# Expert logits as three products: x's part before attention, the projection's part in 8 extra columns, new routing groups

## The chip, the cores and the metric

The kernel runs on 1 core of one Trainium2 chip. The metric is the device time of one launch in microseconds (us). Before the change it is 968.08 us, the median of 3 runs (967.9 to 970.68). The engines are TensorE (PE in the profile, its weight loads PEld), VectorE (DVE), ScalarE (ACT), GpSimd (POOL) and SyncE (SP), which here issues most of the transfers.

## The reference

One layer of attention and a feed-forward part with 8 experts, over 4 x 1024 tokens of width 256, in float32:

```
x2  = x + proj(attention(rope(qkv(layernorm(x)))))       # 16 heads of 16, causal
xn  = layernorm(x2)
aff = xn @ centroids.T                                    # 8 logits for each token
e   = argmax(aff);  alpha = sigmoid(aff[e])
h   = relu((layernorm(xn) * ln_g[e] + ln_b[e]) @ w1[e].T + b1[e])
out = x2 + alpha * (xn + h @ w2[e].T + b2[e]) + (1 - alpha) * xn
```

What matters here is `aff`. The mean of a token is a shift that centred centroids cancel and its standard deviation is a positive factor, so the largest logit can be found from x2 times the centred centroids. As x2 = x + o @ w_proj + b, those logits are the sum of x @ c, o @ (w_proj @ c) and b @ c.

## The kernel before, in words

There are four stages, each a block in which every engine has its own instruction list in program order, tied to the others by semaphores.

**Projection** (`phase_project_attend`, h = 0 to 15): 8 blocks of 512 tokens, two steps h each. x and its transpose x_feat are loaded in rings of three (`xt`, `xf`; `load_x`, `load_features`, XR = 3). PE projects q and k (line 970) and v (line 892), DVE applies the rotation and splits into three bf16 parts together with ACT and POOL; POOL's `part3` is the last part of step h, after which SP's `store(h)` writes the parts to DRAM (line 511). From h = 11 on PE already computes score blocks for the first attention step ("items", `put_item`, line 944), and DVE reduces each to block maxima (line 800). Items 9 to 17 follow after the last step (the drain). There are 18 items for a step; items 11 to 14 are the diagonal ones. SP's loads of the q and k stacks for the attention steps 0 and 1 are spread over h = 5 to 7 and h = 12 to 15.

**Attention** (16 steps of one batch and four heads): the maxima are transposed (line 913), split on DVE (779, 781) and POOL, and stored as extra rows of the stack by SP (line 556); then the scores (line 1004), exponentials on ACT (line 712), masks on POOL (line 636) and the product with v (line 1020). The items of the next step stand between the scores, by a plan written in `ITEM_AT` and `FIRST_AT`. POOL loads the experts' second weights in steps 1, 2, 14 and 15.

**Routing** (`phase_route`): 32 tiles of 128 tokens. For tile n, PE transposes o (line 1404), ACT copies it (`oT`, line 1212), PE adds the bias row (line 1395) and the projection (line 1397) in `ps_p`, and DVE adds x (line 1317). Then PE transposes x2 (line 1418), ACT copies it (`xT`, line 1218) and PE multiplies it by the centred centroids (`ps_a`, line 1427), which were made at the start of the stage (line 1409, DVE 1241). PE's order in iteration n is: bias and projection of tile n+1, transposes of o of tile n+2, transposes of x2 of tile n-1, logits of tile n-2. The tiles are in groups, GROUPS = (8, 8, 8, 4, 4). Per group DVE finds the expert (`one_hot`), PE counts ranks (1434, 1436), DVE makes row numbers (`positions`) and scales; ACT writes the first half of the payload (`scaled`, 1203), DVE the second (`tail`, 1310), and POOL scatters one tile per instruction to its expert's region in DRAM (line 1194). At the end DVE makes the table of slots (lines 1344 to 1381); SP then loads the first expert's weights and, after all scatters, the first rows (line 216). SP also stores pad rows at the regions' ends.

**Experts** (`phase_ffn`): 39 slots of 128 rows, not touched by the change.

## Time and profile before

| what | value |
|---|---|
| median of the runs | 968.08 us (967.9 to 970.68) |
| the profiled execution | 968.24 us, its span 966.3 us |
| mean granted PE clock | 0.962 of 2.4 GHz |
| busy in the span | PE 896.1, DVE 610.3, ACT 532.7, POOL 313.8 us |
| DMA | 130.41 MB, mean 135 GB/s |
| projection, attention, routing, experts | to about 124, to 569, to 670, to 966 us |

The busy time of PE is over 90% of the span, yet this is an average over stages: at the two passages, from projection to attention and from routing to the experts, PE waits for others.
### The profile page before, as it was taken

Reading aid. Unit: us, or ns where it says so; the run is one execution under the profiler, and the core shown is the slowest. Engines: PE = TensorE matmul, PEld = TensorE weight load, DVE = VectorE, ACT = ScalarE, POOL = GpSimd, SP = SyncE. Lnnn points to the kernel's source line nnn. Section 1 sums busy time; section 2 is a strip of 40 time slices with the busy share of each in tenths; the row PEclk is TensorE's granted clock in tenths of the full one; section 3 lists DMA queues with packets and bytes.
Section 4 is the critical chain, followed back from the end, with each engine's and each line's share of the span. In section 5 each row is a group of like instructions: output and inputs, shape, how many; then the busy total and the mean of one; then the engine's idle time right before and its main releaser. Section 6 shows DMA issues by size and latency. Waiting matters only on the chain. (4 is left out here: it accounts for less than half of the span.)

```text
span 966.3 us, 20566 instructions
## 1 busy us (share of the span) xinstructions
PE 896.1 (93%) x6695; PEld 540.2 (56%) x6696; DVE 610.3 (63%) x1107; ACT 532.7 (55%) x1339; POOL 313.8 (32%) x470
## 2 busy tenths in 40 slices
PE   7998769999999999999999879962999999999996
PEld 4554313333333333333333238851999999999996
DVE  5989989888888888888887015772232332332332
ACT  4666428778777778777878834560323223223221
POOL 9987734322233323232233310452011111111111
PEclk9999869999999999999999989985999999999998
DMA  7694543322222211112242036336565665665660
GB/s 258 218 246 162 155 137 120 123 68 68 68 67 67 68 55 52 48 50 68 68 154 88 3 121 197 122 148 202 182 212 188 199 212 185 199 213 186 198 216 7
DMA packets 54891, 130.41 MB, mean 135 GB/s; under 512 B 9761, under 2 KB 30626, under 8 KB 48546
## 3 DMA queue, kind: packets, MB, share of 16 engines
q1 hardware_dynamic: 49234, 107.93, 36.1%
q0 software_dynamic: 5584, 21.54, 5.9%
q8 instruction: 43, 0.70, 0.3%
q14 instruction: 30, 0.25, 0.1%
HBM read 100.95 MB, written 28.48 MB: 134 GB/s over the span
## 5 line engine op out<-in xcount | busy, mean ns | idle before, releaser
L712 ACT ACTIVATE arena<-ps_pair 128x512 f32<-128x512 f32 (+3 forms) x768 | 328.9, 494 | 103.3 <-PE ps_pair L1004 98.7
L800 DVE TENSOR_REDUCE B_block_max<-ps_item 128x8 f32<-128x1024 f32 x288 | 340.6, 1221 | 41.5 <-PE ps_item L944 38.3
L1004 PE MATMUL ps_pair<-q_stack,k_stack 99*128 99x512 bf16 (+7 forms) x768 | 191.0, 333 | 5.2 <-ACT arena L712 2.9
L636 POOL TENSOR_SCALAR_AFFINE_SELECT arena<-arena 128x256 f32<-128x256 f32 x256 | 103.9, 406 | 202.8 <-ACT arena L712 200.5
L1020 PE MATMUL ps_pair<-arena,B_v_quad 128*32 128x512 f32 (+3 forms) x1536 | 163.6, 498 | 1.0 <-ACT B_oacc L726 0.7
L1004 PEld LDWEIGHTS ps_pair<-q_stack,k_stack 99*128 99x128 bf16 (+1 forms) x768 | 54.0, 97 | 187.7 <-ACT arena L712 170.5
L1602 PEld LDWEIGHTS D_ps_h<-D_xT,arena 128*128 128x128 f32 x1248 | 147.9, 195 | 4.7 <-ACT D_xT L1540 2.8
L1602 PE MATMUL D_ps_h<-D_xT,arena 128*128 128x128 f32 x1248 | 148.5, 278 | 2.1 <-ACT D_xT L1540 2.1
L1621 PE MATMUL D_ps_y<-arena,D_hr 128*128 x624 | 141.0, 379 | 0.0
L1531 ACT ACTIVATE D_hr<-D_ps_h,ffn_columns 128x128 f32<-128x128 f32 x156 | 44.5, 368 | 165.1 <-PE D_ps_h L1602 165.1
L1621 PEld LDWEIGHTS D_ps_y<-arena,D_hr 128*128 128x128 f32 x624 | 115.7, 190 | 14.1
L1514 POOL DMA_INDIRECT out<-D_res,D_ids x39 | 38.4, 984 | 262.2 <-issue 200.9
L944 PE MATMUL ps_item<-k_stack,q_stack 64*128 64x128 bf16 (+2 forms) x1280 | 107.0, 269 | 14.6 <-DVE B_block_max L800 9.7
L1561 DVE TENSOR_SCALAR D_hr<-D_ps_h,ffn_columns 128x128 f32<-128x128 f32 x156 | 43.9, 345 | 115.3 <-PE D_ps_h L1602 115.3
L944 PEld LDWEIGHTS ps_item<-k_stack,q_stack 64*128 64x128 bf16 x1280 | 46.6, 96 | 68.7 <-DVE B_block_max L800 31.5
L1576 DVE TENSOR_TENSOR D_y<-D_ps_y,ffn_bias 128x256 f32<-128x256 f32 x39 | 16.6, 425 | 84.1 <-PE D_ps_y L1621 84.1
L1540 ACT ACTIVATE D_xT<-D_ps_x,ffn_columns 128x128 f32<-128x128 f32 x78 | 31.4, 453 | 53.6 <-PE D_ps_x L1611 53.6
L970 PE MATMUL ps_pair<-arena 128*128 128x512 f32 x128 | 57.9, 595 | 0.2 <-DVE arena L768 0.2
L1020 PEld LDWEIGHTS ps_pair<-arena,B_v_quad 128*32 128x32 f32 x1536 | 30.3, 108 | 36.2 <-ACT arena L712 15.8
L1194 POOL DMA_INDIRECT payload<-C_pay,C_posi x32 | 31.3, 978 | 57.9 <-DVE C_pay L1310 37.9
L583 POOL TENSOR_TENSOR arena<-arena 128x512 f32<-128x512 f32 x32 | 48.8, 1542 | 2.2 <-DVE arena L841 2.1
L841 DVE SCALAR_TENSOR_TENSOR arena<-ps_pair,A_bq,arena 128x512 f32<-128x512 f32 x64 | 43.6, 739 | 1.8 <-PE ps_pair L970 1.8
(149 smaller groups left out, 786.8 us busy)
## 6 DMA issues: line engine op xcount, KB each, us to landing
arena<-in_w_exp SPq DMA_DIRECT2D x39, 1024.0 KB, 5.1
qk_parts<-arena SPq DMA_DIRECT2D x32, 384.0 KB, 3.4
q_stack<-qk_parts SPq DMA_DIRECT2D x96, 128.0 KB, 2.9
rows<-payload SPq DMA_DIRECT2D x39, 257.0 KB, 2.7
arena<-in_x SPq DMA_DIRECT2D x16, 512.0 KB, 6.4
k_stack<-qk_parts SPq DMA_DIRECT2D x64, 128.0 KB, 2.9
arena<-in_w_exp POOLq DMA_DIRECT2D x8, 1024.0 KB, 6.6
arena<-in_x_feat SPq DMA_DIRECT2D x8, 512.0 KB, 5.8
```

The costliest lines, as they stand in the source:

```text
L583: pool.tensor_tensor(rot[:, h % 2, c, :], rot[:, h % 2, c, :], ds[:, h % 2, 1 - c, :], op).then_inc(s_rot, 1)
L636: pool.affine_select(out=block_p, in_=block_p, compare_op=ALU.is_ge, fill=0.0, base=0, pattern=[[0, 2], [1, P]], channel_multiplier=-1).th ...
L712: act.activation(pr[s % PR][:, h, 0:QW - off], ps_s[(QH * s + j) % R][:, 0:QW - off], ACT.Exp, scale=scale).then_inc(s_e, 1)
L800: dve.tensor_reduce(bmx[:, g:QH:GH, first:first + 3 * gap + 1:gap], src[:, :, :].rearrange("p c (b n) -> p c b n", n=P), AX.X, ALU.max).th ...
L944: mm = pe.matmul(dst[:, half, at * P:(at + n) * P], qs[rows, r, half, bass.ds(g * SEQ + t * P, P)], ks[rows, r, half, bass.ds(g * SEQ + kb ...
L970: mm = pe.matmul(ps_qk[h % 2][:, c, :], wq[:, k, at:at + P], z[:, g % 2, k, :], start=(k == 0), stop=(k == DC - 1))
L1004: pe.matmul(ps_s[(QH * s + j) % R][:, 0:QW - off], ks[rows, r, half, bass.ds(g * SEQ + kb * P, P)], qs[rows, r, half, bass.ds(g * SEQ + c ...
L1020: mm = pe.matmul(ps_o[32 * h:32 * h + 32, off:QW], vq[:, r, kb, h, :], pr[s % PR][:, h, 0:QW - off], start=(kb == 0), stop=(kb == 4 * c + ...
L1531: act.activation(hr[:, S.ring(2), c, :], ps_h[0][:, c, :], ACT.Relu, bias=col[:, bass.ds(e, 1), 2 * DC + c]).then_inc(s_r[0], 1)
L1561: dve.tensor_scalar(hr[:, S.ring(2), c, :], ps_h[1][:, c - HC, :], col[:, bass.ds(e, 1), 2 * DC + c], 0.0, ALU.add, ALU.max).then_inc(s_r[ ...
L1602: mm = pe.matmul(ps_h[f // HC][:, f % HC, :], w1b[:, r, at:at + P], xT[:, r, c, :], start=(c == 0), stop=(c == DC - 1))
L1621: mm = pe.matmul(ps_y[r][:, :], hr[:, r, c, :], w2s[:, bass.ds(e * W2C + c * DIM, DIM)], start=(c == 0), stop=(c == FC - 1))
```

## The change

1. The centred centroids are made in the projection, in h = 5 (`centroid_means`, `centre_centroids`), and the bias's own logits in h = 6 (`bias_logits`). They become columns 256 to 263 of the bias row.
2. x @ c is computed in `x_logits`, from x_feat, one product of 8 columns per tile and half: tiles 24 to 31 in h = 13, 14, 15 (`X_FIRST`), tiles 0 to 15 behind the drained items 9 to 17 (`X_DRAIN`), tiles 16 to 23 behind the first items of attention step 0 (`X_STEP`). For tiles 0 to 23 the features are loaded a second time (6 more blocks, `AGAIN`), in the same ring of three. ACT copies the logits to `xl`.
3. w_proj @ c (`weight_logits`) goes to columns 256 to 263 of `wp`; its transposed operand is loaded in h = 12.
4. In routing the projection has 264 columns; the transposes of x2, their copies and the logits' products are gone. DVE adds two tiles at once, from a ring of four banks. The groups are (4, 8, 8, 6, 4, 2), and the steps of a group stand one or two iterations earlier. `posi`, `sd` and `mv` have room for all tiles, so their waits for earlier scatters are gone. ACT takes the odd tiles' second payload halves and all from tile 26 on.
5. The pad rows are made by POOL in step 3 and stored by SP in step 4 of attention instead of in routing. The stack loads of attention step 1 move from h = 12..15 to h = 10..13.

```diff
-GROUPS = (8, 8, 8, 4, 4)
+GROUPS = (4, 8, 8, 6, 4, 2)
...
+        ctc = ctx.enter_context(nc.sbuf_tensor("centred_centroids", [P, DC, NE], F32))
+        bcol = ctx.enter_context(nc.sbuf_tensor("b_proj_columns", [P, DC], F32))
+        xl = ctx.enter_context(nc.sbuf_tensor("x_logits", [P, NT, NE], F32))
...
+        def centroid_means(pe, mean, dst):
+
+            for c in range(DC):
+                mm = pe.matmul(dst[:, 0:NE], mean, ct[:, c, :], start=(c == 0), stop=(c == DC - 1))
+            mm.then_inc(s_cs, 1)
+            pe.wait_ge(s_bw, 2)
+            for c in range(DC):
+                mm = pe.transpose(dst[:, NE + c:NE + c + 1], bp[0:1, c * P:(c + 1) * P], ident[0:1, 0:1])
+            mm.then_inc(s_cs, 1)
+
+        def centre_centroids(dve, src):
+            dve.wait_ge(s_cs, 2)
+            dve.tensor_tensor(ctc[:, :, :], ct[:, :, :], src[:, 0:NE].unsqueeze(1).to_broadcast([P, DC, NE]), ALU.subtract).then_inc(s_cc, 1)
+            dve.tensor_copy(bcol[:, :], src[:, NE:NE + DC]).then_inc(s_cc, 1)
+
+        def bias_logits(pe, dst):
+            pe.wait_ge(s_cc, 2)
+            for c in range(DC):
+                mm = pe.matmul(dst[0:1, 0:NE], bcol[:, c:c + 1], ctc[:, c, :], start=(c == 0), stop=(c == DC - 1))
+            mm.then_inc(s_bw, 1)
+
+        def keep_bias_logits(dve, src):
+            dve.wait_ge(s_bw, 3)
+            dve.tensor_copy(bp[:, DIM:DIM + NE], src[0:1, 0:NE]).then_inc(s_bw, 1)
+
+        def weight_logits(pe, w_t, dst):
+
+            for c in range(DC):
+                for o in range(DC):
+                    mm = pe.matmul(dst[:, c * NE:(c + 1) * NE], w_t[:, o, c * P:(c + 1) * P], ctc[:, o, :], start=(o == 0), stop=(o == DC - 1))
+            return mm
+
+        def keep_weight_logits(act, src):
+            return act.activation(wp[:, :, DIM:DIM + NE], src.rearrange("p (c n) -> p c n", c=DC), ACT.Copy)
...
+        AGAIN = 6
+        X_FIRST = {13: range(24, 26), 14: range(26, 29), 15: range(29, 32)}
+        X_DRAIN = (1, 2, 2, 2, 2, 2, 2, 2, 1)
+        X_STEP = {0: 1, MAXT: 2, 1: 2, 2: 2, 3: 1}
...
                 def load_features(g):
-                    if g < NG:
-                        if g >= XR:
+                    if g < NG + AGAIN:
+                        if XR <= g < NG + XR:
                             sp.wait_ge(s_mv, TG * (g - XR + 1))
                             sp.wait_ge(s_z, g - XR + 1)
-                        sp.dma_start(xf[:, g % XR, :, :], x_feat[:, g * QW:(g + 1) * QW].rearrange("(c p) n -> p c n", p=P)).then_inc(s_xf[g % XR], 16)
+                        if g - XR >= AGAIN:
+                            sp.wait_ge(s_xl, TG * (g - XR - AGAIN + 1))
+                        at = g % NG * QW
+                        sp.dma_start(xf[:, g % XR, :, :], x_feat[:, at:at + QW].rearrange("(c p) n -> p c n", p=P)).then_inc(s_xf[g % XR], 16)
...
-                    if h % 2 == 1:
+                    if h % 2 == 1 and h < 12:
                         load_features(h // 2 + XR)
                     if h == 5:
                         for g in range(2):
                             sp.wait_ge(s_st[g], 64)
                     if 5 <= h < 8:
                         load_stack(sp, Step(0), qs, ks, parts_d, s_stk, range(5 * (h - 5), 5 * (h - 4)))
-                    if 12 <= h < 16:
-                        load_stack(sp, Step(1), qs, ks, parts_d, s_stk, range(4 * (h - 12), 4 * (h - 11)))
+                    if 10 <= h < 14:
+                        load_stack(sp, Step(1), qs, ks, parts_d, s_stk, range(4 * (h - 10), 4 * (h - 9)))
+                    if h == 12:
+                        sp.wait_ge(s_bn, tiles_dve(TG * 6))
+                        sp.wait_ge(s_sq, tiles_act(TG * 6))
+                        sp.dma_start(wt, w_proj_out.rearrange("(c p) n -> p c n", p=P)).then_inc(s_wt, 16)
+                    if h in (14, 16):
+                        load_features(NG + h // 2 - 6)
+                for g in range(NG + 3, NG + AGAIN):
+                    load_features(g)
...
+                            if i.const == 0:
+                                next_x_logits(X_STEP.get(item, 0))
+                                if item == max(u for u in X_STEP if u != MAXT):
+                                    pe.wait_ge(s_wt, 16)
+                                    weight_logits(pe, wt, ps_o[:, TG * AGAIN * NE:(TG * AGAIN + DC) * NE]).then_inc(s_wx, 1)
+
+                def x_logits(t, g, dst):
+
+                    if t % TG == 0 and g >= NG:
+                        pe.wait_ge(s_xf[g % XR], 16 * (g // XR + 1))
+                    for c in range(DC):
+                        mm = pe.matmul(dst, xf[:, g % XR, c, t % TG * P:(t % TG + 1) * P], ctc[:, c, :], start=(c == 0), stop=(c == DC - 1))
+                    mm.then_inc(s_xl, 1)
...
+                    if h == min(X_FIRST):
+                        pe.wait_ge(s_z, NG)
+                    for t in X_FIRST.get(h, ()):
+                        x_logits(t, t // TG, ps_bc[:, (t - TG * AGAIN) * NE:(t - TG * AGAIN + 1) * NE])
...
+                pe.wait_ge(s_xe, 1)
+                pe.wait_ge(s_pr, 4 * NH)
+                x_tiles = iter(range(TG * AGAIN))
+
+                def next_x_logits(count):
+                    for t in [next(x_tiles) for _ in range(count)]:
+                        x_logits(t, NG + t // TG, ps_o[:, t * NE:(t + 1) * NE])
+
                 for item in range(DRAIN, UNITS):
                     put_item(Step(-1), item)
+                    next_x_logits(X_DRAIN[item - DRAIN])
...
+                for n in range(NT + 4):
+                    if n < NT and n % 2 == 1:
+                        u, at = n // 2, (n - 1) % R
+                        two = xx[n // G][:, n % G - 1:n % G + 1, :]
                         dve.wait_ge(s_pj, n + 1)
                         dve.wait_ge(s_x[2 * n // G], 16)
-                        dve.tensor_tensor(xx[n // G][:, n % G, :], ps_p[n % 2][:, :], xx[n // G][:, n % G, :], ALU.add).then_inc(s_x2, 1)
+                        dve.tensor_tensor(two, ps_p[:, at:at + 2, 0:DIM], two, ALU.add).then_inc(s_x2, 1)
+                        dve.tensor_tensor(xl[:, n - 1:n + 1, :], ps_p[:, at:at + 2, DIM:DIM + NE], xl[:, n - 1:n + 1, :],
...
-                for n in range(-2, NT + 5):
+                for n in range(-2, NT + 4):
                     t = n + 1
                     if 0 <= t < NT:
                         pe.wait_ge(s_ot, t + 1)
-                        if t >= 2:
-                            pe.wait_ge(s_x2, t - 1)
-                        pe.matmul(ps_p[t % 2][:, :], ones3[:, :], bp3[:, :], start=True, stop=False)
+                        if t >= R:
+                            pe.wait_ge(s_x2, (t - R) // 2 + 1)
+                            pe.wait_ge(s_lg, (t - R) // 2 + 1)
+                        pe.matmul(ps_p[:, t % R, 0:DIM + NE], ones3[:, :], bp3[:, :], start=True, stop=False)
                         for c in range(DC):
-                            mm = pe.matmul(ps_p[t % 2][:, :], oT[:, t % R, c, :], wp[:, c, :], start=False, stop=(c == DC - 1))
+                            mm = pe.matmul(ps_p[:, t % R, 0:DIM + NE], oT[:, t % R, c, :], wp[:, c, :], start=False, stop=(c == DC - 1))
                         mm.then_inc(s_pj, 1)
...
-                    if n == -1:
-                        pe.wait_ge(s_ones, 1)
-                        for c in range(DC):
-                            mm = pe.matmul(ps_k[:, 0, :], ones[:, :], ct[:, c, :], start=(c == 0), stop=(c == DC - 1))
-                        mm.then_inc(s_cs, 1)
-                        pe.wait_ge(s_pre, 5)
-                        pe.wait_ge(s_cc, 1)
-                    t = n - 1
-                    if 0 <= t < NT:
-                        pe.wait_ge(s_x2, t + 1)
-                        pe.wait_ge(s_zt, t)
-                        for c in range(DC):
-                            mm = pe.transpose(ps_z[:, c * P:(c + 1) * P], xx[t // G][:, t % G, c * P:(c + 1) * P], ident)
-                        mm.then_inc(s_tz, 1)
-                    t = n - 2
-                    if 0 <= t < NT:
-                        g, r, i = place(t)
-                        pe.wait_ge(s_zt, t + 1)
-                        if g >= 2:
-                            pe.wait_ge(s_hot, g - 1)
-                        for c in range(DC):
-                            mm = pe.matmul(ps_a[r][:, i, :], xT[:, t % R, c, :], ctc[:, c, :], start=(c == 0), stop=(c == DC - 1))
-                        mm.then_inc(s_af, 1)
-                    for g in after(n, 4):
+                    for g in after(n, 3):
                         k = GROUPS[g]
+                        if g == 0:
+                            pe.wait_ge(s_pre, 5)
                         pe.wait_ge(s_hot, g + 1)
                         pe.wait_ge(s_sn, g)
                         every = hot[:, g % 2, :, :]
...
```

SP's list at the end of the projection, before. `store(h)` is a pair of `qk_parts` rows; `A_part3` is POOL's last part; the last row is the first of the maxima's rows (lines 235 to 249 load the stack):

```order
L511 DMA qk_parts<-arena 128x3x512 [waits A_part3]
L511 DMA qk_parts<-arena 128x3x512
L240 DMA k_stack<-qk_parts 32x1x2048
L235 DMA q_stack<-qk_parts 32x1x2048
L240 DMA k_stack<-qk_parts 32x1x2048
L244 DMA q_stack<-qk_parts 32x1x2048
L511 DMA qk_parts<-arena 128x3x512 [waits A_part3]
L511 DMA qk_parts<-arena 128x3x512
L249 DMA k_stack<-qk_parts 16x2048 x2
L511 DMA qk_parts<-arena 128x3x512 [waits A_part3]
L511 DMA qk_parts<-arena 128x3x512
L556 DMA q_stack<-B_nm 3x16x128 [waits B_max_part3]
```

The same place after the change; line 564 is `load_features`, and `A_x_logits` counts the tiles of x_logits that PE has finished:

```order
L571 DMA qk_parts<-arena 128x3x512 [waits A_part3]
L571 DMA qk_parts<-arena 128x3x512
L564 DMA arena<-in_x_feat 128x2x512 [waits A_x_logits,A_z_ready,A_v_projected]
L571 DMA qk_parts<-arena 128x3x512 [waits A_part3]
L571 DMA qk_parts<-arena 128x3x512
L571 DMA qk_parts<-arena 128x3x512 [waits A_part3]
L571 DMA qk_parts<-arena 128x3x512
L564 DMA arena<-in_x_feat 128x2x512 [waits A_x_logits,A_z_ready,A_v_projected]
L564 DMA arena<-in_x_feat 128x2x512 [waits A_x_logits] x3
L624 DMA q_stack<-B_nm 3x16x128 [waits B_max_part3]
```

The first feature load shown is the second block that is loaded again (tiles 4 to 7); the one after the last store is for tiles 8 to 11, and three more follow before the maxima's rows.

PE's list in the drain, after the change, from the end of item 12 to item 15 (line 1025 and 1036: items, line 1057: x_logits, two instructions per tile; before, the rows of 1057 are absent):

```order
L1057 MATMUL ps_pair<-centred_centroids,arena 128x8 x4
L1025 MATMUL ps_item<-B_mask_right,B_mask_left 128x4x64 x4
L1036 MATMUL ps_item<-k_stack,q_stack 128x128 x8
L1057 MATMUL ps_pair<-centred_centroids,arena 128x8 x4
L1025 MATMUL ps_item<-B_mask_right,B_mask_left 128x4x64 x4
L1036 MATMUL ps_item<-k_stack,q_stack 128x128 x8
L1057 MATMUL ps_pair<-centred_centroids,arena 128x8 x4
L1036 MATMUL ps_item<-k_stack,q_stack 128x256 x4
```

Behind item 13, the second pair of rows, stand tiles 7 and 8, and behind item 14 tiles 9 and 10.

PE's list in the routing loop, one iteration before and a little more (`C_ps_o` the transposes of o, `C_ps_z` those of x2, `C_ps_a` the logits):

```order
L1395 MATMUL C_ps_p<-b_proj_rows,ones_rows 128x256
L1397 MATMUL C_ps_p<-w_proj,C_oT 128x256 x2
L1404 MATMUL C_ps_o<-cst,arena 128x128 x2
L1418 MATMUL C_ps_z<-cst,arena 128x128 x2
L1427 MATMUL C_ps_a<-C_centred,C_xT 128x8 x2
L1395 MATMUL C_ps_p<-b_proj_rows,ones_rows 128x256
```

And after, two iterations:

```order
L1492 MATMUL C_ps_p<-b_proj_rows,ones_rows 128x264
L1494 MATMUL C_ps_p<-w_proj,C_oT 128x264 x2
L1501 MATMUL C_ps_o<-cst,arena 128x128 x2
L1492 MATMUL C_ps_p<-b_proj_rows,ones_rows 128x264
L1494 MATMUL C_ps_p<-w_proj,C_oT 128x264 x2
L1501 MATMUL C_ps_o<-cst,arena 128x128 x2
```

The bias row of a tile now stands directly behind the transposes of the same tile's o.

## Rows read from the trace of the kernel before

**Rows 1.** The page's head: the span.
```profile
span 966.3 us, 20566 instructions
```

**Rows 2.** Table by stage: stretch, its length, busy by engine, PEclk, DMA share, GB/s.
```profile
105.00:560.00 455.00, 437.57 (x3930) 154.47 (x3930) 372.15 (x381) 344.50 (x798) 148.15 (x333) 0.97 0.25 78
...
640.00:672.00 32.00, 4.68 (x39) 3.72 (x37) 15.18 (x70) 8.92 (x22) 16.18 (x18) 0.61 0.56 190
```

**Rows 3.** Timeline of the passage to attention: start, us, engine, line, what.
```profile
112.19 11.61 DVE L800 TENSOR_REDUCE B_block_max<-ps_item 128x8 f32<-128x1024 f32 x10 [0.49 <-PE ps_item L944]
...
118.81 4.20 POOL L578 TENSOR_TENSOR arena<-arena 128x1024 bf16<-128x1024 f32 x2
...
119.32 0.61 PE L944 MATMUL ps_item<-k_stack,q_stack 64*128 64x256 bf16 x4 [0.20 <-DVE B_block_max L800]
...
123.63 1.11 SPq L511 DMA_DIRECT2D qk_parts<-arena  x2
...
124.28 0.21 DVE L809 COPY B_mx<-B_max_of_blocks 128x96 f32<-128x96 f32 x1
...
125.70 0.61 PE L944 MATMUL ps_item<-k_stack,q_stack 64*128 64x512 bf16 x2 [3.51 <-DMA k_stack<-qk_parts]
...
127.56 0.28 DVE L779 TENSOR_SCALAR B_n<-ps_item 96x128 bf16<-96x128 f32 x1
...
133.04 0.58 PE L1004 MATMUL ps_pair<-q_stack,k_stack 99*128 99x512 bf16 x1 [1.67 <-DMA q_stack<-B_nm]
```

**Rows 4.** The line of load_features (504), 8 loads: from issue to landing.
```profile
DMA to landing us min/median/max: 4.8/5.8/11.3
```

**Rows 5.** The same table for three stretches with the clock.
```profile
112.00:124.00 12.00, 6.87 (x80) 3.63 (x76) 11.78 (x11) 4.62 (x6) 9.89 (x7) 0.60 0.47 143
...
571.50:578.40 6.90, 6.11 (x20) 4.32 (x19) 2.24 (x7) 0.77 (x2) 0.00 (x0) 0.51 1.06 347
...
582.00:640.50 58.50, 58.49 (x393) 50.17 (x392) 40.93 (x164) 30.72 (x84) 16.36 (x19) 1.00 0.41 141
```

**Rows 6.** Timeline of the routing loop at full clock, one period.
```profile
585.14 0.28 PE L1395 MATMUL C_ps_p<-b_proj_rows,ones_rows 3*128 3x256 bf16 x1
...
586.32 0.38 PE L1404 MATMUL C_ps_o<-cst,arena 128*128 128x128 f32 x2
...
586.53 0.38 PE L1418 MATMUL C_ps_z<-cst,arena 128*128 128x128 f32 x2
...
586.74 0.38 ACT L1212 ACTIVATE C_oT<-C_ps_o 128x256 f32<-128x256 f32 x1 [1.40 <-PE C_ps_o L1404]
586.75 0.51 PE L1427 MATMUL C_ps_a<-C_centred,C_xT 128*128 128x8 f32 x4
...
587.20 0.28 PE L1395 MATMUL C_ps_p<-b_proj_rows,ones_rows 3*128 3x256 bf16 x1
```

**Rows 7.** Timeline of routing at half clock: centroid sums and one period.
```profile
572.55 0.86 PE L1409 MATMUL C_ps_k<-centroids,C_ones 128*128 128x8 f32 x4
...
577.00 0.39 PE L1395 MATMUL C_ps_p<-b_proj_rows,ones_rows 3*128 3x256 bf16 x1 [0.48 <-ACT C_oT L1212]
...
579.19 0.63 PE L1404 MATMUL C_ps_o<-cst,arena 128*128 128x128 f32 x2
...
580.30 0.39 PE L1395 MATMUL C_ps_p<-b_proj_rows,ones_rows 3*128 3x256 bf16 x1
```

**Rows 8.** Timeline of routing's tail: last projection, scatters, table, rows.
```profile
639.55 1.13 PE L1397 MATMUL C_ps_p<-w_proj,C_oT 128*128 128x256 f32 x4
...
640.07 0.97 POOL L1194 DMA_INDIRECT payload<-C_pay,C_posi  x1 [2.93 <-ACT C_pay L1203]
...
658.44 0.33 DVE L1381 SCALAR_TENSOR_TENSOR slot_tab<-C_es,C_ends 1x39 int32<-1x39 f32 x1
...
659.81 0.96 POOL L1194 DMA_INDIRECT payload<-C_pay,C_posi  x1 [0.30 <-issue]
...
667.21 1.45 SPq L216 DMA_DIRECT2D rows<-payload  x2
```

More of the change, by code:

```diff
@@ L1128, in phase_route, with pay_free, of, by_act @@
         s_tab = sem("slot_table")
-        s_pad = sem("pad_rows_written")
         s_fl = sem("ffn_loaded")
-        def place(t):
-            g = group_of[t]
-            return g, g % 2, t - starts[g]
-        def pay_free(eng, t):
-            if t >= RP:
-                eng.wait_ge(s_sc[group_of[t - RP]], 16 * GROUPS[group_of[t - RP]])
+        def pay_free(eng, first, last):
+            for g in sorted({group_of[t - RP] for t in range(first, last) if t >= RP}):
+                eng.wait_ge(s_sc[g], 16 * GROUPS[g])
+        def of(g):
+            return slice(starts[g], starts[g + 1])
+        def by_act(t):
+            return t % 2 == 1 or t >= starts[LAST - 1]
+        def tails_act(n):
+            return sum(by_act(t) for t in range(n))
         pace = [min(2, 1 + g // 2) for g in range(NG)]
         copied_at = [starts[group_of[t] + 1] + 4 + (t - starts[group_of[t]]) // pace[group_of[t]] for t in range(starts[LAST])]
-        assert copied_at == sorted(copied_at)
+        assert copied_at == sorted(copied_at) and copied_at[-1] < NT + 4
         def after(n, m):
@@ L1325, in _ @@
                     for g in after(n, 3):
                         second_scale(g)
-                    for g in after(n, 5):
                         positions(g)
-                    for t in [t for t in range(starts[LAST]) if copied_at[t] == n]:
+                    for t in [t for t in range(starts[LAST]) if copied_at[t] == n and not by_act(t)]:
                         tail(t)
-                    if n < NT:
-                        g, r, i = place(n)
-                        dve.wait_ge(s_bn, n + 1)
-                        dve.bn_aggr(mv[:, r, i, :], st[:, n % R, :]).then_inc(s_v, 1)
@@ L1336, in _ @@
-                tails = iter(range(starts[LAST], NT))
-                def next_tail():
-                    for t in [next(tails, None)]:
-                        if t is not None:
-                            tail(t)
+                    if n < NT and n % 2 == 1:
+                        for t in (n - 1, n):
+                            dve.wait_ge(s_bn, t + 1)
+                            dve.bn_aggr(mv[:, t, :], st[:, t % R, :]).then_inc(s_v, 1)
                 dve.wait_ge(s_sn, NG)
@@ L1385, in _ @@
             def _(pe):
[L1386 removed]
                 pe.wait_ge(s_b3, 16 * NSPLIT)
[L1389 removed]
+                for n in range(-2, NT + 4):
                     t = n + 1
```

241 lines of the change are left out of this document (128 added, 113 removed).

## The prediction

> **What bounds the kernel now.** I read the page first, then the table by stage, then the timeline at the two hand-overs. The span is 966.3 us, the profiled execution took 968.24 us, 1.9 us lie around the span, and the median of the runs is 968.08 us [rows 1]; all sums are made against 968.24. In attention the reader is to see PE busy 437.57 of 455 us: a delay before the first scores isn't worked off there [rows 2]. In routing, from 582 on PE is busy 58.49 of 58.50 us and DVE 40.93, at one tile per 2.06 us [rows 5, 6], and from 640 to 672 PE has almost nothing: POOL's scatters and the chain behind them set that stretch [rows 2, 8]. The expert stage is not touched. So two places count: the hand-over from projection to attention, and the routing loop with its tail.
>
> **Hand-over to attention: what is added.** The logits of x need 32 tiles of x_feat times centred centroids on PE, 8 of them in the steps h = 13 to 15, 16 among the drained items 9 to 17, 8 among the first items of the next step, then the product with the projection's weights. The features of tiles 0 to 23 are loaded a second time, in 6 loads of 512 KB into a ring of three. The order of SP shows it: the load for group 2 (tiles 8 to 11) stands behind store(15), and store(15) waits for POOL's last part. In the trace before that part ends at 118.81 + 4.20 = 123.01; the store went at 123.63 only because stack loads were in SP's queue, and these now stand earlier [rows 3]. Two stores cost 1.1, so this load is issued at 124.1. A feature load lands 4.8 to 11.3 us after its issue, 5.8 in the median [rows 4]: it is there at 129.9 (bounds 128.9 and 135.4).
>
> The page "DMA: Bandwidth & Descriptors" of the Trainium skill (Anatomy of one DMA) gives a fixed part of about 2.0 us and the bytes at 436 GB/s; by that an estimate for 512 KB is 3.2 us and the wait would end 2.6 us sooner. This case's eight loads never took under 4.8 [rows 4], so the trace doesn't bear it out for this queue, and the sum doesn't use it.
>
> PE comes to tile 8 after item 13, where it is at about 118 us today: DVE reduces 10 items from 112.19 to 123.80, one per 1.16 us, and each needs PE's item [rows 3]. PE is in order, so items 14 to 17 stand behind the tile that waits for the load. Behind it stand in PE's queue, up to the first scores: 16 tiles (8 to 23), the weight logits (worth 2 tiles), item 14 (diagonal, worth 2 items), items 15 to 17, items 0 to 4 of the next step, and the maxima's transpose. The clock was 0.60 in the mean from 112 to 124 with PE busy 6.87 of 12 us [rows 5], and up to 129.9 PE now has less to do than then, so I price them at half clock: a product with an 8-column result (the centroid sums) took 0.86 per tile [rows 7], an item 0.61 [rows 3], the transpose 0.5. Sum: 18 x 0.86 + 10 x 0.61 + 0.5 = 22.1 us. First scores at 129.9 + 22.1 = 152.0, against 133.04: +19.0. The other chain, by DVE, is hidden under it: 0.9 + 1.2 until item 14, 4 x 1.16, 0.7 for the maxima (124.28 + 0.21 less 123.80), 1.16 for item 0, and 133.04 - 127.56 = 5.5 from the first copy of the maxima to the scores, 14 us in all. The wait of 3.51 us for the stack in front of item 0 goes [rows 3]; it would give 1.5 us alone, but now it is inside the longer wait. At full clock PE's sum is 11 us and DVE's chain of 14 decides: 128.9 + 14 = 142.9, +9.9. With the latest landing it is 135.4 + 22.1, +24.5. I take +19.0, since the clock was at half in these very rows.
>
> The smaller edits there: 8 tiles at 0.45 each in h = 13 to 15 (the interval from 586.75 to 587.20 [rows 6]) are 3.6 us of PE beside a DVE that is busy throughout, and the products for centroid means and bias in h = 5 and 6 some 1 us. They only count as far as they delay POOL's last part; nought to 4.6, I take +0.5, since DVE is the engine that is waited for. The pad rows (9 stores) and the bias rows lie in attention, where the DMA has room: 0. Without that cover they would stand at the start of routing, as today, where nothing waits for them before the table: 0 again.
>
> **Routing loop.** Removed per tile: two transposes of x2, the four short products, ACT's second copy. What is left on PE is bias row, projection (now 264 columns) and the transposes of the next tile. Taking their starts off the rows gives 2.06 - 0.45 - 0.22 = 1.39 us, but the sum isn't the period. Bias row t starts only when ACT has copied the transposes of t, and those now stand immediately before it in PE's queue. Read it off at full clock: bias at 585.14, transposes at 586.32, ACT's copy at 586.74 for 0.38, next bias 587.20 [rows 6]: 1.18 + 0.88 = 2.06. Today the 0.88 is filled by x2's transposes and the logits; afterwards it is empty, and stays. With 8 more columns in five passes (+0.03) the period is 2.09: over 27 full-clock periods +0.8. At half clock the same loop is 577.00 to 579.19 to 580.30, 3.30 us, before and after [rows 7].
> The first projection of tile 1 no longer waits for the centred centroids: -0.5.
>
> **Tail.** After the last projection (639.55) POOL has 16 scatters left, from 640.07 on, one per 0.96 + 0.30 = 1.26 us, the last at 659.81 for 0.96 (end 21.2 us behind the start of the last projection), and SP loads rows at 667.21 [rows 8]. With the new groups 12 are left (tiles 20 to 31). They start after the last products of that tile (1.0) and DVE's positions of their group, which I put at 3.0 behind: 3.0 + 12 x 1.26 + 0.6 for the short copies between groups = 18.7 against 21.2, so -2.5. The slot table ended at 658.44 + 0.33 [rows 8]; without tails in it and without the wait for posi it comes slightly earlier too. Since the wide weight load moves forward with the table and shares the DMA with the last scatters, I take -2.0; bounds -5 and +2 (DVE now has two group chains behind the last tile).
>
> Sum: +19.0 + 0.5 + 0.8 - 0.5 - 2.0 = +17.8. 968.24 + 17.8 = 986.0 us.
>
> **Rivals.**
> A. The clock stays at half in routing. From 571.5 to 578.4 PE did what every period does afterwards (projection, transposes, wait for ACT) and had 0.51 of the clock although busy 6.11 of 6.9; it rose at 582, after x2's transposes had begun to fill the gap [rows 5, 7]. Each further period costs 3.30 - 2.06 = 1.24. If the rank products of the first group raise it, 4 periods: 991. If nothing does, 27 periods: 1019. Against it: these matmuls are wide ones and the clock may not fall at all. In that case 4 slow periods go too, -5: 981.
> Here the page "TensorE: Matmul & The Clock Gate" of the Trainium skill (A second HAM failure mode: psum-queue depth-cycling) says that short idles between groups of matmuls make the clock oscillate. By that rule rival A would be the forecast; the trace shows the loop with idle in it (0.48 us at 577.00) only at half clock and never at full, so it bears the rule out for not rising and is silent on falling [rows 7].
> B. The hand-over is cheap: the tiles keep the clock full and the load lands at its minimum, +9.9, and routing starts at full clock, -5 - 2 - 0.5 + 0.8: 971. For it: 8 more tiles of PE work before 112. Against: the 5 us and more of idle before tile 8.
> C. Faster. The second loads are in time, so nothing waits at tile 8. Then 24 tiles are hidden under DVE's 1.16 per item, the stack's wait goes (-1.5) and routing gives -1.7: 965. It decides by landing before about 118 us; 129.9 speaks against it, and the order of SP.
>
> **How the numbers follow.** Forecast 0.57 (986, by itself 977 to 993, the clock in routing falling or not), A 0.22, B 0.14, C 0.07. The range leaves out C and the last third of A: 971 to 1012. A difference under 0.3% (2.9 us) can't be told from none here. Faster by more: 0.06, C. Within: 0.03. Slower: 0.91.
>
> **What would show it.** Right: PE's longest wait before the first scores is one for in_x_feat, ending near 130; first scores near 152; 0.5 of the clock up to there; in routing the bias row waits for ACT's copy in each tile, 2.09 apart at full clock; POOL's last scatter some 19 us behind the start of the last projection. Wrong: tile 8 at 118 without a wait for a DMA (then C), or bias rows 1.4 to 1.7 apart in routing, which would mean that the copy is not in the loop's chain.

## The result: 1017.25 us against 968.93 us, 5% slower

The changed kernel takes 1017.25 us (median of 4 runs, 1015.29 to 1017.71), the kernel before, run beside it, 968.93 us (4 runs, 967.9 to 970.68): ratio 1.0493, 95% interval 1.047 to 1.0516. Predicted were 986 us and 971 to 1012: the side was right, the size was not, and the range ended 5 us too early.

The head of the page after, with PE's busy share and its clock in 40 slices of 25.4 us (tenths):

```profile
span 1014.8 us, 20338 instructions
...
PE   7997979999999999999999878884599999999996
...
PEclk9999858999999999999999965555799999999999
```

The span is 48.5 us longer than in [rows 1]. The five slices around 0.5 (23 to 27, counted from 0) are the routing stage; before, only its ends were at half [rows 2, 5]. Where the 48.5 us went is found at three starts: the first scores, the first transposes of routing, and the first transposes of the experts. The timeline of PE before, at the last two (the first scores are the last row of [rows 3]):

```profile
569.84 0.41 PE L1404 MATMUL C_ps_o<-cst,arena 128*128 128x128 f32 x2 [1.59 <-PEq L489]
...
670.21 0.66 PE L1611 MATMUL D_ps_x<-cst,rows 128*128 128x128 f32 x2 [20.94 <-PEq L1148]
```

The timeline after, from POOL's last parts over the wait at tile 8 (PE, line 1057) to the last projection, the last scatter and the experts:

```profile
122.59 4.20 POOL L650 TENSOR_TENSOR arena<-arena 128x1024 bf16<-128x1024 f32 x2
...
127.86 10.88 SPq L564 DMA_DIRECT2D arena<-in_x_feat  x4
133.06 1.02 PE L1057 MATMUL ps_pair<-centred_centroids,arena 128*128 128x8 f32 x4 [6.00 <-DMA arena<-in_x_feat]
...
134.98 1.87 PE L1057 MATMUL ps_pair<-centred_centroids,arena 128*128 128x8 f32 x8
...
154.68 0.61 PE L1125 MATMUL ps_pair<-q_stack,k_stack 99*128 99x512 bf16 x1
...
589.82 0.41 PE L1501 MATMUL C_ps_o<-cst,arena 128*128 128x128 f32 x2 [1.45 <-PEq L546]
...
694.29 2.13 PE L1494 MATMUL C_ps_p<-w_proj,C_oT 128*128 128x264 f32 x4
...
711.63 0.96 POOL L1306 DMA_INDIRECT payload<-C_pay,C_posi  x1 [0.30 <-issue]
...
719.84 0.69 PE L1687 MATMUL D_ps_x<-cst,rows 128*128 128x128 f32 x2 [17.80 <-DMA rows<-payload]
```

| place | before | after | later by |
|---|---|---|---|
| POOL's last part ends | 123.01 | 126.79 | 3.8 |
| first scores | 133.04 | 154.68 | 21.6 |
| routing starts | 569.84 | 589.82 | 20.0 |
| last projection starts | 639.55 | 694.29 | 54.7 |
| experts start | 670.21 | 719.84 | 49.6 |
| span | 966.3 | 1014.8 | 48.5 |

So 20.0 us stem from the hand-over (21.6 at the first scores; attention itself took 1.7 us less in this profile), 34.8 from the routing loop (69.71 to 104.47 us from its first transposes to the last projection), and the tail gives back 5.1 (30.66 to 25.55). One period of the loop after, deep in the stage, and the table from the end of attention on:

```profile
640.27 0.40 PE L1492 MATMUL C_ps_p<-b_proj_rows,ones_rows 3*128 3x264 bf16 x1 [0.48 <-ACT C_oT L1327]
...
640.60 2.13 PE L1494 MATMUL C_ps_p<-w_proj,C_oT 128*128 128x264 f32 x4
...
642.52 0.63 PE L1501 MATMUL C_ps_o<-cst,arena 128*128 128x128 f32 x2
...
643.19 0.38 ACT L1327 ACTIVATE C_oT<-C_ps_o 128x256 f32<-128x256 f32 x1 [2.98 <-PE C_ps_o L1501]
...
643.63 0.39 PE L1492 MATMUL C_ps_p<-b_proj_rows,ones_rows 3*128 3x264 bf16 x1 [0.48 <-ACT C_oT L1327]
```

```profile
560.00:589.00 29.00, 24.12 (x182) 1.00 0.00 1
589.00:600.00 11.00, 8.29 (x23) 0.62 0.87 272
600.00:690.00 90.00, 78.50 (x212) 0.50 0.21 79
```

(The columns of this one are length, PE busy, PEclk, DMA share, GB/s.) The clock is at 1.00 up to the first transposes of routing and falls with the first tile; in the kernel before it fell there too, and came back at 582 [rows 5]. After the change it doesn't come back. The loop has exactly the chain that was predicted, bias row behind ACT's copy behind the transposes, but 3.36 us long, which is the half-clock period of [rows 7] (3.30) with wider products, from the second tile to the last.

### The profile page after: what moved, and what is told of

The parts are those of the page before. It is cut to its first block and busy times, and to the rows that moved or that the text cites. A ratio compares the mean times of both kernels' runs of the same rounds, so it can differ in the third digit from the quotient of the medians.

```text
span 1014.8 us, 20338 instructions
## 1 busy us (share of the span) xinstructions
PE 932.3 (92%) x6598; PEld 561.7 (55%) x6647; DVE 603.2 (59%) x1110; ACT 534.3 (53%) x1331; POOL 314.3 (31%) x471
## 5 line engine op out<-in xcount | busy, mean ns | idle before, releaser
L1125 PE MATMUL ps_pair<-q_stack,k_stack 99*128 99x512 bf16 (+5 forms) x720 | 181.8, 329 | 10.9 <-ACT arena L800 5.6
L1494 PE MATMUL C_ps_p<-w_proj,C_oT 128*128 128x264 f32 x128 | 67.4, 681 | 0.0
L1327 ACT ACTIVATE C_oT<-C_ps_o 128x256 f32<-128x256 f32 x32 | 12.3, 383 | 76.8 <-PE C_ps_o L1501 76.8
```

The costliest lines, as they stand in the source:

```text
L1125: pe.matmul(ps_s[(QH * s + j) % R][:, 0:QW - off], ks[rows, r, half, bass.ds(g * SEQ + kb * P, P)], qs[rows, r, half, bass.ds(g * SEQ + c ...
L1494: mm = pe.matmul(ps_p[:, t % R, 0:DIM + NE], oT[:, t % R, c, :], wp[:, c, :], start=False, stop=(c == DC - 1))
```

## Experiments

Six questions were put to the chip. "ahead" and "wide" are versions of the changed kernel that later ones build on.

### 1. Is it the empty place in the loop that keeps the clock down?

```diff
                         mm.then_inc(s_to, 1)
+                        if 0 <= n < NT:        # filled_ten: 0 <= n < 10
+                            for c in range(DC):
+                                pe.transpose(ps_f[:, c * P:(c + 1) * P], v_all[:, t, c * P:(c + 1) * P], ident)
```

> The changed kernel with two idle transposes (the same form and cost as the transposes of x2 that the change removed; their result is thrown away) put behind the transposes of o in every tile of routing. The chain bias row, projection, transposes, ACT's copy is as long as before. Theory G (the empty 0.9 us before each bias row is what keeps the clock at half): the granted clock returns to 1.00 within about 5 tiles, bias rows stand 2.1 us apart, 28 tiles save 1.26 us each, 35 us: about 982 us. Rival L (the clock of this stage is set by something else, such as the narrower work or the state in which attention ends): bias rows stay 3.35 us apart, 1017 to 1020 us.

Measured: 984.95 us (983.72 to 986.73), ratio 1.0146 (1.0102 to 1.019). Work was added and the kernel became 32 us faster than the changed one. A period of PE in this kernel (line 1506 is the added work):

```profile
640.79 0.28 PE L1493 MATMUL C_ps_p<-b_proj_rows,ones_rows 3*128 3x264 bf16 x1 [0.26 <-ACT C_oT L1328]
641.00 1.16 PE L1495 MATMUL C_ps_p<-w_proj,C_oT 128*128 128x264 f32 x4
642.00 0.38 PE L1502 MATMUL C_ps_o<-cst,arena 128*128 128x128 f32 x2
642.22 0.38 PE L1506 MATMUL C_ps_f<-cst,arena 128*128 128x128 f32 x2
642.86 0.28 PE L1493 MATMUL C_ps_p<-b_proj_rows,ones_rows 3*128 3x264 bf16 x1 [0.26 <-ACT C_oT L1328]
```

The period is 2.07 us. The filling doesn't lengthen the chain, since PE would have waited for ACT there anyway. Theory G holds, L falls: with the place filled the clock comes back, with nothing else changed.

> As filled_loop, but the two idle transposes stand only in the iterations 0 to 9 of routing. Theory H (as the forecast assumed: the clock once up stays up, since the matmuls are wide): as filled_loop, about 983 us. Theory F (the loop without filling cannot hold the full clock either): some 5 tiles at full clock, then 0.50 again within a few tiles; 5 x 1.26 = 6 us saved, about 1011 us.

Measured: 984.22 us (983.12 to 987.43), ratio 1.0144 (1.0097 to 1.019): as fast as with all tiles filled. The table of stretches (length, busy PE, PEld, DVE, ACT, POOL, then PEclk, DMA share, GB/s):

```profile
590.00:598.00 8.00, 7.00 (x21) 4.35 (x20) 1.68 (x10) 1.15 (x3) 0.00 (x0) 0.57 0.85 282
598.00:622.00 24.00, 20.54 (x106) 14.37 (x104) 13.57 (x60) 9.21 (x22) 3.20 (x4) 1.00 0.46 160
622.00:659.00 37.00, 27.60 (x144) 18.86 (x144) 24.07 (x108) 19.14 (x47) 16.96 (x21) 1.00 0.31 118
```

In the last stretch nothing is filled any more, PE is busy 27.60 of 37 us, and the clock stays at 1.00. The same loop without filling from the start was busy 78.50 of 90 us and never left 0.50. So both levels hold themselves in this loop once its first tiles are through. It is not the clock at the entry that decides: the changed kernel enters at 1.00, and the clock falls in its first tile. What raises it again here is seen at the first filled tile, not after 5 as was expected; the bias row behind it already takes 0.28 us, as at full clock, where the one before took 0.40:

```profile
596.71 0.64 PE L1506 MATMUL C_ps_f<-cst,arena 128*128 128x128 f32 x2
597.40 0.28 PE L1493 MATMUL C_ps_p<-b_proj_rows,ones_rows 3*128 3x264 bf16 x1
```

H holds, F falls.

### 2. What is the loop worth if the copy is taken out of the chain?

```diff
-                for n in range(-2, NT + 4):
-                    t = n + 2
+                for n in range(-3, NT + 4):
+                    t = n + 3
```

(once for ACT's copies, once for PE's transposes; PE's bias row stays at n + 1)

> The changed kernel with the transposes of o and ACT's copy one tile further ahead in routing (tile n+3 instead of n+2), so that ACT's copy lies beside the next projection and not between transposes and bias row. Theory G: no gap, full clock, PE's own sum of 1.42 us or DVE's 1.5 us per tile sets the period; 32 x (3.35 - 1.5) = 59 us less, the tail a little shorter: about 960 us. Rival L (the clock stays at half whatever fills the gap): PE's sum at half clock 0.40 + 2.13 + 0.64 less overlaps = 3.0 us per tile, 11 us less, about 1006 us.

Measured: 970.98 us (969.27 to 974.16), ratio 1.0017 (0.9998 to 1.0037), 46 us less than the changed kernel and level with the kernel before. A period of PE:

```profile
610.11 0.28 PE L1492 MATMUL C_ps_p<-b_proj_rows,ones_rows 3*128 3x264 bf16 x1
610.33 1.16 PE L1494 MATMUL C_ps_p<-w_proj,C_oT 128*128 128x264 f32 x4
611.32 0.38 PE L1501 MATMUL C_ps_o<-cst,arena 128*128 128x128 f32 x2
611.63 0.28 PE L1492 MATMUL C_ps_p<-b_proj_rows,ones_rows 3*128 3x264 bf16 x1
```

The period is 1.52 us and the wait for ACT is gone. In this profile the clock stays at 1.00 at the start of routing. The loop doesn't depend on that: in early_loads (experiment 4), with the same loop, it falls to 0.50 there (584 to 586) and is back at 1.00 from 588 on.

The total is 11 us above the expectation. The loop gave 55.3 us (104.47 to 49.12) instead of 59, and the tail doesn't shrink with it: from the last projection (639.98) to the experts (671.04) it takes 31.1 us instead of 25.6. Two things lengthen it. From the second group on (621.33) POOL's scatters follow each other at about 1.40 us apiece, so the last starts at 663.24, later than the loop would let it; that bound was missing in the sum. And once among them POOL stands still, because DVE does (the row at 645.33 in experiment 4):

```profile
648.55 0.97 POOL L1306 DMA_INDIRECT payload<-C_pay,C_posi  x1 [4.43 <-ACT C_pay L1318]
```

Without such a stop the tail of the same loop is 28.6 us (early_loads, 633.79 to 662.37).

### 3. What does the hand-over cost?

```diff
 def x_logits(t, g, dst):
-                    if t % TG == 0 and g >= NG:
-                        pe.wait_ge(s_xf[g % XR], 16 * (g // XR + 1))
+                    if g >= NG:          # one_x_tile: if t != 24
+                        return
...
```

(Both kernels also leave out the second loads of the features, and copy the missing logits from the tiles that remain, so their tokens go to other experts.)

> The changed kernel without the x logits of tiles 0 to 23 (their values are copied from those of tiles 24 to 31, so the routing of these tokens is another one) and without the second loads of their features: the hand-over alone is priced. The 8 products in h = 13 to 15 and the weight product stay. Theory: no wait for a DMA, first scores at 133.0 + 3.8 (POOL's last part is that much later in the trace after) - 1.5 = 135 us instead of 154.7; 18 to 19 us less at the end, about 999 us. Rival (attention works off part of the delay, so the tiles cost less than they seem): first scores at 135 but routing starts only 10 us sooner, about 1007 us.

Measured: 999.58 us (998.48 to 1001.32), ratio 1.0302 (1.0258 to 1.0346): 17.7 us less than the changed kernel. First scores:

```profile
134.93 0.59 PE L1125 MATMUL ps_pair<-q_stack,k_stack 99*128 99x512 bf16 x1 [0.23 <-DMA q_stack<-B_nm]
```

The theory holds within 1 us: the 24 tiles and their loads cost 19.8 us at the first scores and nearly all of it at the end.

> As no_x_tiles, and of the 8 tiles in h = 13 to 15 only tile 24 is multiplied (the x logits of all tokens are copied from it, so the routing of tokens is another one). Theory (PE is on the path in h = 13 to 15, so these 8 products and not the small edits in h = 5 and 6 or the moved stack loads make POOL's last part 3.8 us late): POOL's last part ends 7 x 0.45 = 3.2 us earlier than in no_x_tiles, about 996.5 us. Rival (the other edits make it late): as no_x_tiles, 999.5 us.

Measured: 997.49 us (995.25 and 999.74), ratio 1.0311 (1.0279 to 1.0343). The total moves by less than these few runs can tell apart; the trace of POOL's last parts can:

```profile
119.16 4.21 POOL L650 TENSOR_TENSOR arena<-arena 128x1024 bf16<-128x1024 f32 x2
```

They start at 119.16, against 121.62 in no_x_tiles, 122.59 in the changed kernel and 118.81 in [rows 3]. In this pair the products of h = 13 to 15 make 2.5 us, where 3.2 were expected. It is one profile of each, though, and profiles differ here by themselves: four with the changed kernel's list up to this place (its own, filled_loop, filled_ten and ahead) have 121.82 to 122.59, and three profiles of one kernel in experiment 6 have 118.12, 119.25 and 120.54. So the pair points to the products, but doesn't fix their price, nor what the other edits cost.

### 4. Does SP's order make the wait at tile 8?

```diff
+                    if h == 15:
+                        load_features(NG + 2)
+                        load_features(NG + 3)
                     if h >= 1:
                         store(h - 1)
```

(on ahead; the two loads are taken out of their old places)

> The kernel ahead with the feature loads for tiles 8 to 11 and 12 to 15 issued in front of store(14) instead of behind store(15). Theory (the order of SP's queue makes the wait at tile 8): the load is issued near 117.5, when tile 31's product frees its buffer, and lands near 123.5, before PE comes to tile 8; the 6.0 us of idle go, first scores at 149 instead of 154.6, about 965 us. Rival (DVE's chain or a later load takes its place): less than 2 us gained, 969 us or more. The clock stays at 0.50 from 120 on by both.

Measured: 960.86 us (960.24 to 962.94), ratio 0.9939 (0.9922 to 0.9957). The first scores come at 148.38, 6.3 us before those of the changed kernel (154.68; ahead has 154.63) but still 15.3 us behind those of the kernel before, and PE is busy without a break before them; first the table for 120 to 140 (columns as above), then the scores in the timeline:

```profile
120.00:140.00 20.00, 20.00 (x133) 17.42 (x129) 10.94 (x13) 2.54 (x3) 7.80 (x7) 0.50 0.50 159
```

```profile
148.38 0.61 PE L1128 MATMUL ps_pair<-q_stack,k_stack 99*128 99x512 bf16 x1
```

The theory holds for the place: the order of SP's queue makes the wait. The wait is the smaller part of the delay, however; the 15.3 us that remain are PE's own work, without a gap and at half clock. The total fell by 10 us, but the kernel before was faster beside this run as well (967.73 against 969.36 us beside ahead), so by the ratios 7.5 us are gained, where some 6 were expected. In the profiled runs routing is also 1.4 us shorter, and in ahead DVE stood still once behind the last projection, which this kernel doesn't show:

```profile
645.33 0.21 DVE L1401 TENSOR_TENSOR C_rank<-C_ps_k,C_seen 128x48 f32<-128x48 f32 x1 [4.80 <-remote]
```

What it waited for stays open. The stop belongs to the execution and not to a kernel: on the same line DVE stands 4.9 us in wide_again and 4.6 in wide_third, and not at all in wide, which are three profiles of one kernel (experiment 6).

As this run's expectation had it, but against the reason that the prediction gave, the clock is 0.50 while PE is busy 20.00 of 20.00 us. The changed kernel shows the same before its wait for the load: PE is busy all the time, and the clock goes down, to 0.50 from 121 on (the columns are those of the table for 120 to 140).

```profile
120.00:124.00 4.00, 4.00 (x37) 3.53 (x36) 2.43 (x3) 1.75 (x3) 3.49 (x2) 0.57 0.00 0
```

### 5. Is it the narrow products that let the clock fall there?

```diff
+                    if g >= NG:
+                        pe.transpose(ps_s[0][:, 0:P], xf[:, g % XR, 0, t % TG * P:(t % TG + 1) * P], ident)
                     for c in range(DC):
```

> As early_loads, with one idle 128x128 transpose added in front of each of the 24 x products of the drain and of attention step 0. Theory N (the 8-column products, although PE is busy all the time, are what lets the clock fall): with wider work between them the clock is 1.00 for most of 120 to 145, a tile costs 0.45 + 0.22 = 0.67 us instead of 0.93 and an item 0.39 instead of 0.61; 24 x 0.26 + 8 x 0.22 = 8 us less than early_loads, about 957 us, although work was added. Rival (the clock is down for another reason): 24 x 0.43 = 10 us more than early_loads, about 975 us.

Measured: 963.33 us (961.36 to 965.93), ratio 0.9959 (0.9942 to 0.9976), some 2 us more than early_loads, which the intervals hardly tell from none; the first scores come at 150.69, 2.3 us later. The clock:

```profile
120.00:140.00 20.00, 20.00 (x142) 17.49 (x138) 10.35 (x11) 2.55 (x4) 7.40 (x5) 0.50 0.50 160
```

Theory N falls as it was put: a 128-column transpose in front of each tile doesn't bring the clock back. The rival had the clock right and the price wrong, since the added 24 x 0.43 cost only about 2 us. What holds the clock at half with PE fully busy is not settled. That it goes with the stretch of 8-column products is only seen, not shown: in the changed kernel, in early_loads and in early_loads_filled the clock is back at 1.00 only behind the first scores, from 159, 154 and 155 on. In the kernel before, which has none of these products, it comes back at 139, also behind the first scores, but there PE had stood idle before them.

### 6. The x logits the other way round

```diff
-                    for c in range(DC):
-                        mm = pe.matmul(dst, xf[:, g % XR, c, t % TG * P:(t % TG + 1) * P], ctc[:, c, :], ...)
+                    for c in range(DC):
+                        for j in range(TG):
+                            mm = pe.matmul(dst[32 * j:32 * j + 32, :], ctcw[:, c, :], xf[:, g % XR, c, j * P:(j + 1) * P],
+                                           start=(c == 0), stop=(c == DC - 1), tile_position=(0, 32 * j))
...
+        X_FIRST = {7: 3, 9: 4, 10: 5, 13: 6, 15: 7}
+        X_DRAIN = {9: 0, 11: 1, 13: 2}
```

> The kernel ahead with the x logits made the other way round: the centred centroids (8 columns, padded to 32) are the stationary operand and four tiles of x_feat (128 columns each) run side by side in the four column groups of the array, 8 matmuls for 512 tokens; the result, experts by tokens, is copied and transposed by PE, four transposes for 16 tiles. Groups 3 to 5 are done in h = 7, 9, 10 from the first load, 6 and 7 in h = 13 and 15, only groups 0 to 2 are loaded again, all before store(14); the weight product stands behind item 12. Theory: PE's part for 4 tiles is about 0.5 us at full clock (rows of the product with v: 8 records of 128 columns 0.43 us) instead of 1.8, no wait for a DMA is left, first scores near 134 instead of 154.6, 20 us less than ahead: about 951 us. Rival (ACT's copies and the transposes form a chain of their own before the first scores, or the three groups in h = 7 to 10 delay POOL): 3 to 5 us worse, about 955 us.

Measured: 947.17 us (944.74 to 950.14), ratio 0.9788 (0.9759 to 0.9817); two repetitions (below) gave 0.9778 and 0.9761. This is 70 us less than the changed kernel and 2.1 to 2.4% less than the kernel before; nothing of the computation is left out. PE in the drain (1070: 4 tiles, 1123: turning 16 tiles' logits back) and the first scores:

```profile
114.01 0.64 PE L1070 MATMUL ps_pair<-arena,centred_centroids 128*32 128x128 f32 x16
114.59 0.66 PE L1123 MATMUL ps_pair<-cst,arena 128*128 128x128 f32 x4
...
116.92 0.64 PE L1070 MATMUL ps_pair<-arena,centred_centroids 128*32 128x128 f32 x16 [0.90 <-DMA arena<-in_x_feat]
...
132.49 0.58 PE L1153 MATMUL ps_pair<-q_stack,k_stack 99*128 99x512 bf16 x1 [1.50 <-DMA q_stack<-B_nm]
```

Four tiles cost 0.64 us, against about 2.0 in the old form at full clock, where the changed kernel's three tiles of h = 15 take 1.50. The first scores come 0.6 us before those of the kernel before; the two repetitions have 133.61 and 130.99, so the two kernels are level there. The kernel differs from ahead in more than the form of the product: three blocks are loaded again instead of six, their loads stand earlier, and three blocks are done in h = 7 to 10. What each of these gives was not measured; only the price of the product was.

The Trainium skill's page "TensorEngine Tiling (Array Packing)", section When to Use Tiling, has this as the swap of stationary and streaming operand together with 4x column tiling, for a right side of 32 columns. The trace agrees, and here it is 3.1 times as fast.

The same kernel was run twice more, and with two other sets of groups:

```diff
-GROUPS = (4, 8, 8, 6, 4, 2)
+GROUPS = (4, 6, 6, 6, 6, 4)          # wide_groups_of_6
+GROUPS = (4, 4, 6, 6, 6, 4, 2)       # wide_7_groups
```

> The kernel wide once more, beside two versions of it: 945 to 950 us, ratio 0.979.

> As wide, GROUPS = (4, 6, 6, 6, 6, 4). In wide POOL's 32 scatters set the end of routing: it idles 6.25 us between group 0 (595.86) and group 1 of 8 tiles (603.28), then works without a gap of over 1 us to 641.6. Theory: with 6 tiles group 1 is ready two tiles, 3 us, sooner, and the last scatter goes 3 us sooner, about 944 us. Rival (the last group of 4 has a longer chain behind the last tile, or DVE's steps are late): no gain or 1 to 2 us lost.

> As wide, GROUPS = (4, 4, 6, 6, 6, 4, 2): group 1 is ready four tiles sooner, but DVE has one group's steps more (about 2.5 us) and POOL one more copy. Theory: 3 to 5 us less than wide, about 943 us. Rival: DVE, busy 33.9 of 40 us in the loop of ahead, becomes late and the gain is gone, 947 us.

> The kernel wide a third time, unchanged: two of the six runs of wide_again took 2132 and 2917 us, at a clock of 1.00. If the kernel has a stall of its own, such runs come again; if they came from outside, all runs are 944 to 952 us, ratio 0.978.

Measured, in this order: 943.89 to 952.44 us (ratio 0.9778, 0.9749 to 0.9807), but two further runs of 2132 and 2917 us, which the ratio leaves out; 949.67 us (ratio 0.9799, 0.978 to 0.9819); 945.87 us (0.976, 0.974 to 0.978); 945.91 us (945.26 to 949.6; 0.9761, 0.9734 to 0.9788), without any such stray run. The two strays did not come again in the 5 runs of wide_third, which ran on another chip, so they are taken to come from outside; one repetition makes that likely and doesn't prove it. The groups make no difference that these intervals can tell: the 3 to 5 us that an earlier group 1 was to give don't show. Both theories fell, and their rivals stand. The profiles also differ in the clock at the start of routing, which is worth as much as what was looked for: from the first transposes to the last projection, three profiles of the one kernel wide take 53.4, 53.7 and 50.9 us. The table for 569 to 579 of wide, then of wide_7_groups (the same 10 us have 0.52 in wide_again and 0.97 in wide_third, both the kernel wide):

```profile
569.00:579.00 10.00, 9.81 (x25) 6.13 (x25) 1.69 (x6) 1.60 (x5) 0.00 (x0) 0.50 1.00 317
```

```profile
569.00:579.00 10.00, 10.00 (x46) 7.01 (x47) 4.99 (x19) 2.89 (x8) 0.00 (x0) 1.00 1.01 315
```

## Point by point

1. **Hand-over, +19.0, first scores at 152.0.** Came as 21.6, at 154.68. The chain is as put: SP's order, a wait for in_x_feat, then 21.6 us from tile 8 to the scores against 22.1 predicted. The load took 5.2 us to tile 8, against 5.8; its start was off, 127.86 instead of 124.1. Two readings under it were wrong. PE was to come to tile 8 at about 118 and wait 12 us. The tiles in front of it were left out of that, and it came at 127.06 and waited 6.00; with the wait gone, in early_loads, 15.3 of the 21.6 us are still there. So rival C was wrong in its own case too, since loads in time don't hide 24 tiles under DVE. And half clock was forecast because PE would have less to do. The clock was at half in PE's fullest stretch, before the wait began (the table for 120 to 124 in experiment 4), so the level was right by luck, and its reason wrong.
2. **Small edits upstream, +0.5.** Came as 3.8, within the bounds of 0 and 4.6 but at the wrong end. The 8 products in h = 13 to 15 were taken to lie beside DVE. But PE was on the path: DVE's waits for PE's projections (its line 841 before, 929 after) add up to 1.8 us in the kernel before, 5.8 in the changed one (5.1 to 5.5 in filled_loop, filled_ten and ahead), 5.4 in no_x_tiles and 2.5 in one_x_tile. So the products stand in DVE's way; how much of the 3.8 us is theirs, single profiles don't tell.
3. **Routing loop, +0.8 − 0.5.** This is the step that failed: it came as +34.8. Its period at full clock (2.09) was right, measured 2.07 in filled_loop, whose whole time, 984.95, is near the forecast of 986. What failed is the term under it, that routing would have its 27 full-clock periods. It had none; the periods are 3.36 us each to the end. That is rival A in its full form, priced at 1019 and given 0.22 together with its mild form (the rank products of the first group don't raise the clock). The evidence against A was only "the clock may not fall at all". But it didn't have to fall later on: it had to rise, from first tiles that were at 0.50 in the kernel before as well [rows 5], and the change removes just the work that filled the wait there; filled_loop and filled_ten put it back, and the clock rises. That row was read and then weighed too lightly; cutting the last third of A off the range went against it too.
4. **Tail, −2.0.** Came as −5.1: −2.9 up to the end of the last scatter (18.3 us behind the last projection instead of 21.2, predicted 18.7), and the rows load behind it 2.2 us faster. In filled_loop, from 660.47 to 688.37, the whole tail is 27.9 instead of 30.66, −2.8.
5. **The Trainium skill on the clock.** Its page "TensorE: Matmul & The Clock Gate", section A second HAM failure mode: psum-queue depth-cycling, tells of a kernel in which short idles between groups of matmuls made the clock oscillate. No run here shows an oscillation in the loop. It stays at 0.50 in the changed kernel and at 1.00 in filled_ten, with an idle of 0.48 us in most periods of both.
6. **The Trainium skill on the landing of a load.** Its page "DMA: Bandwidth & Descriptors" has the figures behind the estimate of 3.2 us in the section Anatomy of one DMA, and that section is on transfers issued by GpSimd. The load at tile 8 is issued by SP and took 5.2 us, so the prediction was right to go by its own rows.
